# Attention for 32 batches on one core: every fourth pair of heads scored once, turned by a transfer

## The reference, cut to what matters

```python
x = x + attn(layernorm(x))     # x: 32 batches x 256 tokens x 128; 16 heads of 64
x = x + ffn(layernorm(x))      # hidden 512, ternary weights
# attn, for each batch and head:
q = x Wq / 8;  k = x Wk;  v = x Wv
logits = q k^T                 # 256 x 256
attn = softmax(logits)         # over the keys
out = (attn v, heads put side by side) Wp + bp
```

## Time and profile before

| | |
|---|---|
| three runs | median 992.88 us (992.01 to 993.58) |
| the profiled execution | 992.29 us |
| its span, first to last instruction | 990.5 us |
| busy share of the span | PE 98%, PEld 78%, DVE 86%, ACT 74%, POOL 87% |

### The profile page before, as it was taken

The page is one execution under the profiler, slowest core; times in us unless marked ns, Lnnn a source line. Parts: engine busy times, 40 slices in busy tenths (PEclk is TensorE's granted clock), DMA queues, the critical chain, the costliest instruction groups (busy, mean ns, idle before and its releaser), DMA issues.

```text
span 990.5 us, 39211 instructions
## 1 busy us (share of the span) xinstructions
PE 968.2 (98%) x15932; PEld 767.8 (78%) x15932; DVE 854.4 (86%) x1743; ACT 733.4 (74%) x1180; POOL 861.8 (87%) x849
## 2 busy tenths in 40 slices
PE   7899999999999999999999999999999999989998
PEld 6577777787787887777778878877888887767776
DVE  6898988888888898899888988898888988768787
ACT  4687777778777777777777777777777778677775
POOL 5789898989886999999999999999899999878885
PEclk9999999999999999999999999999999999999999
DMA  6112232342323333223333332233433333367885
GB/s 136 44 31 53 47 74 53 62 64 64 79 43 51 64 84 65 61 51 59 85 63 64 58 83 39 61 61 83 65 63 64 63 64 63 79 126 158 168 171 129
DMA packets 242786, 74.08 MB, mean 75 GB/s; under 512 B 218032, under 2 KB 240304, under 8 KB 242608
## 3 DMA queue, kind: packets, MB, share of 16 engines
q1 hardware_dynamic: 240528, 71.05, 36.7%
q10 hardware_dynamic: 2080, 0.52, 0.3%
HBM read 11.41 MB, written 8.39 MB: 20 GB/s over the span
## 4 chain that ended last, share of the span: by engine, by line
PE 92%; DVE 2%; ACT 2%; issue 1%; DMA 1%; POOL 1%; SPq 0%; DVEq 0%; ACTq 0%; POOLq 0%
PE S L765 11%; PE PV L790 8%; PE M L725 7%; PE PV L792 6%; PE PV L791 6%; PE QK L712 5%; PE QK L714 5%; PE QK L713 5%; PE misc L765 5%; PE S L757 5%; PE M L843 2%; PE M L808 2%; PE M L845 2%; PE M L844 2%; PE misc L757 2%; PE M L810 2%
## 5 line engine op out<-in xcount | busy, mean ns | idle before, releaser
L1325 POOL TENSOR_TENSOR pl<-p 128x1024 f16<-128x1024 f32 x253 | 476.6, 1896 | 33.1 <-ACT p L1102 32.8
L1526 DVE TENSOR_REDUCE negmax<-M 128x4 f32<-128x1024 f32 x252 | 306.7, 1217 | 22.2 <-PE M L725 16.2
L1110 ACT ACTIVATE QKh<-QK 128x512 f16<-128x512 f32 x251 | 149.5, 596 | 142.2 <-PE QK L714 141.4
L1102 ACT ACTIVATE p<-S,s_exp 128x1024 f32<-128x1024 f32 x173 | 192.2, 1111 | 56.9 <-PE S L765 56.3
L790 PEld LDWEIGHTS PV<-V,p 128*128 128x128 bf16 x2048 | 186.6, 98 | 47.1 <-issue 36.3
L790 PE MATMUL PV<-V,p 128*128 128x65 f16 x2048 | 214.8, 193 | 4.5 <-DVE O L1540 3.6
L791 PE MATMUL PV<-V,p 128*128 128x64 f16 x2048 | 213.2, 192 | 0.0
L792 PE MATMUL PV<-V,pl 128*128 128x65 f16 x2048 | 212.5, 194 | 0.0
L1546 DVE TENSOR_TENSOR QKl<-QK,QKh 128x512 f16<-128x512 f32 x251 | 172.3, 687 | 43.3 <-ACT QKh L1110 42.2
L791 PEld LDWEIGHTS PV<-V,p 128*128 128x128 bf16 x2048 | 189.0, 97 | 4.7
L792 PEld LDWEIGHTS PV<-V,pl 128*128 128x128 f16 x2048 | 188.7, 97 | 0.0
(11 more groups left out here) (246 smaller groups left out, 2472.4 us busy)
## 6 DMA issues: line engine op xcount, KB each, us to landing
y_kept<-yTb SPq DMA_DIRECT2D x32, 128.0 KB, 1.7
yT<-y_kept SPq DMA_DIRECT2D x16, 256.0 KB, 3.4
result<-X SPq DMA_DIRECT2D x15, 256.0 KB, 3.0
X<-in_L_attn_query SPq DMA_DIRECT2D x7, 512.0 KB, 4.2
OT<-O SPq DMA_TRANSPOSE x64, 4.1
shift<-negmax SPq DMA_TRANSPOSE x63, 2.3
O<-in_L_attn_Wk ACTq DMA_DIRECT2D x2, 256.0 KB, 4.8
O<-in_L_attn_Wq SPq DMA_DIRECT2D x2, 256.0 KB, 5.6
```

Of the source, the lines that this page charges most:

```text
L1102: e.activation(p32[r][:, :, :, :].rearrange("p i m n -> p (i m n)"), score_bank(p)[:, :], ACT.Exp, scale=s_exp[:, :]).then_inc(s_ex, 1)
L1325: e.tensor_tensor(pl[r][:, :, :, :].rearrange("p i m n -> p (i m n)"), p32[r][:, :, :, :].rearrange("p i m n -> p (i m n)"), p_high(r).rea ...
L1526: e.tensor_reduce(dst[:, :, NB * jj:NB * jj + NB], max_bank(p)[:, :].rearrange("p (i t m) -> p i t m", i=2, t=NB), AX.X, ALU.max, negate=T ...
```

## The change

Pairs with p % 4 == 3 from 87 to 239 (39 of them, two to a batch: at j=3 and j=7) become "direct". They are always the second pair of the double steps j=2 and j=6. A direct pair has no `max_scores`, takes no part in its group's maxima, and has no shift matmuls. `direct_scores` computes its full scores with the queries on the partitions; `direct_max` takes the row maximum of these (DVE); ACT multiplies it to a bias and takes the exponentials in four ACTIVATEs of 128 x 256, since each token block and head has its own bias (`direct_exps`). The result has queries on the partitions and must be turned: ACT copies its high part (`direct_high`), POOL writes its low part (`direct_low`) to a tile `p_rows`, and SP issues a DMA transpose to `p_turned` (`turn_p`), which `weighted` reads. In the rest of the loop the maxima are dealt anew (two to a double step, direct ones counted), and `weighted` comes one pair later: t-3 and t-2 in place of t-2 and t-1. The two new tiles lie in the four `a` buffers, which the FFN uses only later.

The diff, cut; left out are counters that now skip the direct pairs, semaphores, and the two places where the double steps begin and end.

```diff
+DIRECT_0, DIRECT_1 = 87, 240
...
+def direct(p):
+    return p % 4 == 3 and DIRECT_0 <= p < DIRECT_1
...
+def maxima_to(p):
+    return p + 1 - direct_no(p + 1)
...
+def held_back(t):
+    return t % 4 == 2 and TWO_0 <= t and direct(t + MAX_LEAD + 3)
+def two_maxima(t):
+    first = [t + MAX_LEAD - 1] if held_back(t - 2) else []
+    last = [] if held_back(t) or direct(t + MAX_LEAD + 1) else [t + MAX_LEAD + 1]
+    return first + [t + MAX_LEAD] + last
...
+        a_all = sb("a_all", [P, A_RING, F])
...
+        p_rows = a_all[:, 2:4, :].rearrange("p a f -> p (a f)").bitcast(F16).rearrange("p (s c) -> p s c", s=2)
+        p_turned = a_all[:, 0:2, :].rearrange("p a f -> p (a f)").bitcast(F16)
+        neg_rows, bias_rows = sb("neg_rows", [P, 2, NB]), sb("bias_rows", [P, 2, NB])
...
+            def turn_p(p):
+                d = direct_no(p)
+                e.wait_ge(s_dhi, d + 1)
+                e.wait_ge(s_dlo, d + 1)
+                if d:
+                    e.wait_ge(s_pv, p - 3)
+                e.dma_start_transpose(p_turned.rearrange("p (c n) -> p c n", n=P),
+                                      p_rows.rearrange("p s c -> p (s c)")).then_inc(p_in_turned, 16)
...
+                    if t and direct(t - 1):
+                        turn_p(t - 1)
...
+            def direct_scores(p):
+                h, lo = QKh[p % QK_RING], QKl[p % QK_RING]
+                e.wait_ge(s_qklo, p + 1)
+                e.wait_ge(s_ex, p - 1)
+                for t in range(NB):
+                    tok = slice(t * P, (t + 1) * P)
+                    for n, (q, k) in enumerate(((h, h), (lo, h), (h, lo))):
+                        for i in range(2):
+                            rows = head_rows(i)
+                            op = e.matmul(misc_pair[:, i * 512 + t * N:i * 512 + (t + 1) * N], q[rows, 0, tok], k[rows, 1, :],
+                                          start=n == 0, stop=n == 2, skip_group_check=True)
+                            if t == NB - 1 and n == 2:
+                                op.then_inc(s_sc, 1)
...
+            def p_parts(p, i, m, t):
+                if direct(p):
+                    parts = p_turned.rearrange("p (s i t m n) -> p s i t m n", s=2, i=2, t=NB, m=NB)
+                    return parts[:, 0, i, t, m, :].bitcast(BF16), parts[:, 1, i, t, m, :]
+                tok = slice(t * P, (t + 1) * P)
+                return p_high(p % P_RING)[:, i, m, tok], pl[p % P_RING][:, i, m, tok]
...
             def two_steps(t):
                 if t > TWO_0:
                     e.wait_ge(*two_free(t - 2))
-                max_scores(t + MAX_LEAD)
+                max_scores(two_maxima(t)[0])
                 scores(t)
-                scores(t + 1)
-                max_scores(t + 1 + MAX_LEAD)
-                weighted(t - 2)
+                if direct(t + 1):
+                    direct_scores(t + 1)
+                else:
+                    scores(t + 1)
+                for p in two_maxima(t)[1:]:
+                    max_scores(p)
+                weighted(t - 3)
                 queries_keys(t + Q_LEAD + 1)
                 for piece in two_values(t):
                     values(*piece)
                 if two_project(t):
                     project_tile(*two_project(t), t)
-                weighted(t - 1)
+                weighted(t - 2)
                 queries_keys(t + Q_LEAD + 2)
...
+            def direct_exps(p):
+                r, d = p % P_RING, direct_no(p)
+                e.wait_ge(s_dmx, d + 1)
+                e.activation(bias_rows[:, :, :], neg_rows[:, :, :], ACT.Identity, scale=s_exp[:, :]).then_inc(s_dbias, 1)
+                e.wait_ge(s_dbias, d + 1)
+                if d:
+                    e.wait_ge(s_dlo, d)
+                else:
+                    e.wait_ge(s_pv, p - P_RING + 1)
+                for i in range(2):
+                    for t in range(NB):
+                        op = e.activation(p32[r][:, i, t, :], misc_pair[:, i * 512 + t * N:i * 512 + (t + 1) * N], ACT.Exp,
+                                          scale=s_exp[:, :], bias=bias_rows[:, i, t:t + 1])
+                op.then_inc(s_ex, 1)
...
+            def direct_high(p):
+                d = direct_no(p)
+                e.wait_ge(s_ex, p + 1)
+                if d:
+                    e.wait_ge(p_in_turned, 16 * d)
+                e.activation(p_rows[:, 0, :].bitcast(BF16), p_high(p % P_RING).rearrange("p i m n -> p (i m n)"),
+                             ACT.Copy).then_inc(s_dhi, 1)
...
-                exps(t + 1)
+                if not direct(t + 1):
+                    exps(t + 1)
                 qk_high(t + Q_LEAD + 1)
+                if direct(t + 1):
+                    direct_exps(t + 1)
...
                 qk_high(t + Q_LEAD + 2)
+                if direct(t + 1):
+                    direct_high(t + 1)
...
+            def direct_low(p):
+                r, d = p % P_RING, direct_no(p)
+                e.wait_ge(s_ex, p + 1)
+                if d:
+                    e.wait_ge(p_in_turned, 16 * d)
+                e.tensor_tensor(p_rows[:, 1, :], p32[r][:, :, :, :].rearrange("p i m n -> p (i m n)"),
+                                p_high(r).rearrange("p i m n -> p (i m n)"), ALU.subtract).then_inc(s_dlo, 1)
...
+            def direct_max(p):
+                d = direct_no(p)
+                e.wait_ge(s_sc, 2 * p + 2)
+                if d:
+                    e.wait_ge(s_dbias, d)
+                e.tensor_reduce(neg_rows[:, :, :], misc_pair[:, :].rearrange("p (i t m) -> p i t m", i=2, t=NB),
+                                AX.X, ALU.max, negate=True).then_inc(s_dmx, 1)
...
+                max_out(two_maxima(t)[0])
                 qk_low(t + MAX_LEAD + 1)
-                max_out(t + MAX_LEAD + 1)
-                sums_inverse(t - 2)
-                normalise(t - 2)
+                if direct(t + 1):
+                    direct_max(t + 1)
+                for p in two_maxima(t)[1:]:
+                    max_out(p)
+                sums_inverse(t - 3)
+                normalise(t - 3)
...
-                sums_inverse(t - 1)
-                normalise(t - 1)
+                sums_inverse(t - 2)
+                normalise(t - 2)
```

More of the change, by code:

```diff
@@ L87, in in_two, with direct_no @@
     return TWO_0 <= t < TWO_1
+def direct(p):
+    return p % 4 == 3 and DIRECT_0 <= p < DIRECT_1
+def direct_no(p):
+    return sum(direct(k) for k in range(p))
+def maxima_to(p):
[6 more added lines that the diff above has]
+    return first + [t + MAX_LEAD] + last
 def weighted_pair(t):
-    return t - PV_LAG if 0 <= t - PV_LAG < NP and t != TWO_1 else None
+    return t - PV_LAG if 0 <= t - PV_LAG < NP else None
 def max_pairs(t):
@@ L149, in low_on_pool_before @@
 def low_on_pool_before(p):
-    return p - sum(d < p for d in LOW_ON_DVE)
+    return p - sum(d < p for d in LOW_ON_DVE) - direct_no(p)
 def shift_group(t):
@@ L384, in layer @@
         yT = [sb(f"yT{i}", [P, FG, 2, P], F16) for i in range(Y_RING)]
-        a = [sb(f"a{i}", [P, F]) for i in range(A_RING)]
+        a_all = sb("a_all", [P, A_RING, F])
+        a = [a_all[:, i, :] for i in range(A_RING)]
+        p_rows = a_all[:, 2:4, :].rearrange("p a f -> p (a f)").bitcast(F16).rearrange("p (s c) -> p s c", s=2)
+        p_turned = a_all[:, 0:2, :].rearrange("p a f -> p (a f)").bitcast(F16)
+        neg_rows, bias_rows = sb("neg_rows", [P, 2, NB]), sb("bias_rows", [P, 2, NB])
         zTh = [sb(f"zTh{i}", [P, FC, P], BF16) for i in range(3)]
@@ L419, in layer @@
         s_sc, s_ex, s_pl, s_pl_dve = sem("s_scores"), sem("s_exp_done"), sem("s_p_lo"), sem("s_p_lo_dve")
+        s_dmx, s_dbias, s_dhi, s_dlo, p_in_turned = (
+            sem(f"s_direct_{n}") for n in ("max", "bias", "p_hi", "p_lo", "p_transposed"))
         s_pv, s_rs, s_o = sem("s_pv"), sem("s_rsum"), sem("s_o")
@@ L720, in max_scores @@
                 if p >= 2:
-                    e.wait_ge(s_mx, p if p >= FIRST else p - 1)
+                    e.wait_ge(s_mx, maxima_to(p - 1) if p >= FIRST else p - 1)
                 for t in range(NB):
@@ L747, in scores @@
                 elif p == PAIRED:
-                    e.wait_ge(s_mx, NP)
+                    e.wait_ge(s_mx, maxima_to(NP - 1))
                 elif p > PAIRED:
@@ L768, in scores @@
                                 op.then_inc(s_sc, 1)
+            def direct_scores(p):
[17 more added lines that the diff above has]
+                return p_high(p % P_RING)[:, i, m, tok], pl[p % P_RING][:, i, m, tok]
             def weighted(p):
                 b, j = divmod(p, HP)
-                r = p % P_RING
-                ph = p_high(r)
-                if p in LOW_ON_DVE:
+                if direct(p):
+                    e.wait_ge(p_in_turned, 16 * (direct_no(p) + 1))
+                elif p in LOW_ON_DVE:
                     e.wait_ge(s_pl_dve, LOW_ON_DVE.index(p) + 1)
@@ L784, in weighted @@
                 for t in range(NB):
-                    tok = slice(t * P, (t + 1) * P)
                     for i in range(2):
```

(32 more changed lines are left out.)

2 lines of the change are left out of this document (1 added, 1 removed).

## The result

The changed kernel took 1005.24 us (median, 1004.63 to 1006.51) beside 992.68 us for the kernel before in the same runs: ratio 1.013 (95% interval 1.0117 to 1.0143), 12.6 us slower. The profiled execution spans 1002.8 us, 12.3 more than before.

The account below looks back on a forecast made before the run. PE bounded the kernel before; ACT's list was to hold PE at the end of j=4. 19 x 0.85 us lost less 20 x 0.31 won gave +10 us, so 1003 us, range 984 to 1014.

Parts of the forecast that it names:

- PE's saving: On PE, a direct pair loses shift matmuls and maxima: 0.44 us each, 17.2 us for 39 pairs.
- ACT's prices: Costs on ACT per direct pair: four exponentials 0.48 us each, bias 0.30, `direct_high` 0.96, removed 1.00; sum 2.18 us.
- The walk: ACT's list from T, PE's start of j=2: `qk_high` of j=4 at T+11.34, 0.85 us lost, 19 times.
- the place of PE's wait: PE's wait for DVE's `v_low` was to grow from 0.3 us to about 1.5 after j=4.
- The lag: `weighted` one pair later makes `exps` wait at j=0 and j=4; costed at nothing, about 0.3 us at each if uncovered.
- The cover: At j=0 and j=4, added ACT work was to push the exponential behind the `weighted` it waits for, hiding about 0.3 us.
- The walk at j=0: ACT's list over j=6 and j=0, without `y_norm`: 0.13 of PE's 0.44 us lost, 0.31 won, 20 times.
- The transfer rival: The direct pair's transpose lands too late for `weighted` in j=6: 39 us on top, about 1035; chance 0.07.
- ACT's busy share: ACT's busy time in the changed stretch was to rise from 75.5% to about 92%.
- The total: Whole kernel: 19 x 0.85 us lost less 20 x 0.31 won, +10 us, giving 1003 us.

Follow-up runs that it names:

- e11: Changed kernel with `y_norm` moved from the end of j=2 to j=0, `direct_low` ahead of `norm_root` on POOL, and five `p32` and `pl` tiles instead of four: 977.4 us.
- e5: Kernel before with two more ACTIVATEs of 128 x 512 (1.0 us of ACT, output unused) at the end of j=2, ahead of `y_norm`: 1008.7 us, ratio 1.0156.
- e4: Changed kernel with `y_norm` (1.22 us of ACT) moved from the end of j=2 to the end of j=0: 992.8 us, ratio 1.0005.
- e6: Kernel before with two more ACTIVATEs of 128 x 512 (output unused) at the end of j=6, where no `y_norm` follows: 993.6 us, ratio 1.0004.
- e1: Changed kernel without any direct pair, so only `weighted` coming one pair later is left: 1005.2 us, ratio 1.0123.
- e10: Changed kernel with rings of five `p32` and `pl` tiles instead of four: 998.0 us, ratio 1.0051.

## Why the prediction was right, and where it was not

**PE's saving.** Sized at 0.44 us a direct pair, 17.2 us in all. e11 shows 0.95 a batch for two pairs, 0.47 each, and a gain of 15.7 us (993.04 - 977.37). The price was right and slightly low; 19 x 0.95 are 18.1, so some 2.4 us of the gain are lost outside these batches.

**ACT's prices.** The exponential of 128 x 256 was put at 0.48 in a row: 502.84 - 501.03 is 1.81 for four, 0.45 each, below the 0.48; its mean length is 0.56, estimated 0.59. Bias 0.32 (0.30), `direct_high` 0.95 (0.96), `y_norm` 1.24 (1.22).

**The walk.** `qk_high` of j=4 was forecast at T+11.34 and came at T+11.26; the first `qk_high` at T+3.45 to the hundredth. From `qk_high` of j=4 to PE's restart I took 2.69 from before; it was 2.57. It is 2.57 in e5 too, which is why e5 cost 0.79 a batch and not 0.9:

```profile
510.96 0.59 ACT L1110 ACTIVATE QKh<-QK 128x512 f16<-128x512 f32 x1
513.53 0.39 PE L725 MATMUL M<-QKh 64*128 64x256 f16 x4 [0.37 <-DVE V L1555]
```

Before, DVE's `qk_low` starts at 504.13 (below) and its two `v_low` end at 506.13, 2.00 for the three; after, it is 1.89.

```profile
504.13 0.69 DVE L1546 TENSOR_TENSOR QKl<-QK,QKh 128x512 f16<-128x512 f32 x1 [0.34 <-ACT QKh L1110]
```

The likely reason is that both `v_high` follow each other directly now, so that DVE no longer waits for the second; such a wait would be too short to be listed, so this is not shown. j=2 with j=4 lost 0.65, not 0.85. The experiments e4, e5 and e6 show that it is this list that binds.

I had the place of PE's wait wrong, though: I forecast about 1.5 us for `v_low` after j=4. PE stops earlier, 0.62 us for `qk_low` ahead of `queries_keys` inside j=4, and then 0.36 for `v_low`.

**The lag, costed at nothing.** This step failed. I wrote that the exponential "has been pushed behind this point anyway" by ACT's work, and "about 0.3 us at each" without that cover. The price was right: 0.29 at each, by e1. The cover was there at j=4 only. At j=0, without `y_norm` ahead, the changed kernel waits 0.27 us for the weighted product (13 times in the waits above), and e10 gets 0.30 a batch back. That is 20 x 0.29 = 5.8 us of loss that I had not in the sum.

**The walk at j=0.** My 0.31 won there was 0.18, but not for the reason that I gave. I had ACT's list take back 0.13 of PE's saving. Without the lag it takes back nothing: in e10 j=0 starts at 539.51, and

```profile
543.46 0.63 ACT L1200 ACTIVATE QKh<-QK 128x512 f16<-128x512 f32 x1
```

so `qk_high` comes 3.95 us after it, 4.02 by my walk. I compared with 3.89, which is the value of j=2. In the kernel before, j=0 has its own, 516.67 - 512.73 = 3.94:

```profile
516.67 0.60 ACT L1110 ACTIVATE QKh<-QK 128x512 f16<-128x512 f32 x1 [0.49 <-PE QK L714]
```

So j=6 with j=0 would win 0.47, and the lag takes 0.29 of it.

**Luck.** The batch came out at 26.82 for a forecast of 26.9 because errors cancel: 5.8 us of lag that I left out, against 3.8 too much at j=4 (19 x 0.20), 2.6 too much from ACT at j=0 (20 x 0.13) and 0.6 too little saved at j=6 (20 x 0.03). ACT's list at j=4 was the right bound and carries most of the loss; that the sum fits to about 1 us is luck.

**The transfer rival.** Room of 1.5 us was forecast with ACT holding PE, 0.2 without. For the pairs at j=3 whose transfer takes the usual 4.3 us it is 0.95 in the changed kernel and 0.13 in e4. So a transfer is late in two batches of the changed kernel (1.0 us), and in seven of 19 once `y_norm` is moved. It lands 4.4 us after issue (median; 4.3 to 6.2), 4.1 was taken. The risk was real, the size of the rival (39 us) was not; and 39 us on top of 1003 are 1042, not the 1035 that I wrote.

**ACT's busy share.** Forecast above 90%, measured 86 to 87. The 92% divided by the old batch length; over 26.82 us the same sum is 90%. The rest, about 1 us a batch, is probably that older instructions now follow each other directly too, and busy time counts their overlap of 0.11 us once; I did not add it up.

**The total.** 1003 against 1005.2; the late transfers and the two ends of the stretch, 2.5 us together, stand in no sum of mine. (The upper end of my range, 1014, is more than the third of the way to 1028 that I gave as its reason, which is 1011; the measured time lies below both.)

## What to carry to other kernels

Before work is moved to an engine that is "a quarter idle", find the stretch of its list that somebody waits for, and add the work up there; the same microsecond in each batch cost 15.6 us in one place and nothing in another. When a consumer is moved later, every ring that its completion frees has to be checked for the producer that now waits inside the same step: one more buffer turned a 12 us loss into nothing. Several delays can hide one behind the other (here ACT's list, the transfer, the ring), so an edit that removes the first shows less than it is worth until the next is gone. And a forecast that comes out right in total should be checked term by term: cutting the batch into its double steps showed here what the total hid.

## What the runs showed that I had not expected

The DMA transposes of 128 x 2048 raised the DMA share from a third to 54 to 60%, yet most instructions of DVE, ACT and POOL kept their mean lengths from 300 to 960 us: POOL's subtraction 1895 ns before and 1896 after (`direct_low` 1895), `qk_low` on DVE 686 in both, the exponential from `S` 1109 and 1114. The largest growth, 482 to 513 ns for `xn<-X,nm,r`, is there in e5 as well (514), which has no added transfer. Two `v_high` became shorter as a pair, 1.25 us before and 1.10 after: ACT comes later than PE's values there, so the second follows the first without a gap.
